# Fusion block on one core: GpSimd's row ids in four steps, a reciprocal on VectorE, and two VectorE steps put elsewhere in the turn

## The chip, the cores and the metric

The kernel runs on one core of one Trainium2 chip. The metric is the device time of one execution in microseconds. Engines are named as the profile names them: PE is TensorE, DVE is VectorE, ACT is ScalarE, POOL is GpSimd, SP is SyncE.

## What is computed

The reference is one transformer block over 16 images with 128 text rows each; all arithmetic is fp32.

```python
h = tokenize(x)                      # 64 patches of 28x28x3 and a class row, times pos_embed
h = concatenate([h, txt], axis=1)    # 16 x 193 x 128
h = h + attn(layernorm(h))           # linear attention, elu + 1, rotation, 1/z, 3-tap conv
h = h + ffn(layernorm(h))            # 8 experts, each row goes to 2, and one shared expert
# in ffn:
scores = xt @ gate_w.T
_, idx = top_k(scores + biases, 2)
p = sigmoid(top_k(scores, 2)[0]);  p = p / sum(p)
```

With e1 = exp(-s1) and e2 = exp(-s2) the two shares are (1 + e2) and (1 + e1), each over (2 + e1 + e2). So a row needs two exponentials, one sum and one reciprocal.

## The kernel before, in words

The 16 images are worked on in G = 8 groups of two. A group has three row tiles of 128 rows (one of patches, two of text); one more tile holds all class rows. Each engine runs one instruction list, written out by hand, and engines wait for each other on counting semaphores. A waiting instruction holds up everything behind it on its engine.

The program has three stages. In the first, the loop `for i in range(1, G - 1)` on DVE (line 1125), ACT (643) and PE (1542) works one *turn* per group: group i is projected and attended, group i-1 gets its second norm (`second_rows`, `second_stats`), and group i-2 is routed. The last group follows behind the loop, in a *tail* that also starts the shared expert (`shared_up`, `shared_down`) and splits the expert weights into a rounded part and a remainder (`remainder_w13`). In the second stage PE runs 56 expert tiles, one after the other; in the third the results come back and are added.

What the change touches in a turn of DVE:

- `turn_parts(i)` and `turn(i)` (lines 942 and 951) build the rotated features `rr` with three instructions over 128x768: two products (L947, L949) and their sum (L956). PE's `sums` (L1450, L1452) waits for the sum.
- `patch_rows(i+1)` (L915) takes the next group's patch tokens out of PE's bank; `patch_stats(i+1)` (L890, L894) takes their mean and variance. From there the path is ACT `rstd1` (L522, L524), DVE `mean1` (L900), ACT `norm_patches` (L555) and, behind that on ACT, `key_sums` (L550), for which PE's `attend` (L1464) waits.
- `positions(i-2)` (L1052) sums the places of group i-2's rows in the expert buffers.
- `attended` and `mixed` (L987, L992) end the attention of group i-1; `elu_most(i)` (L933) opens group i.

POOL works group by group. `goals(g)` writes the ids of the rows, `shares(g)` their weights (groups 0 to 5 only; `EARLIER` is 6), and then six indirect DMAs (L861; eight for the last group) scatter the rows to `xs_dram`. Inside `goals` and `shares` every step waits for the one ahead of it through `then_pool`, which counts them on `pool_chain`, 7 to a group (`WEIGHED`). ACT's `chances(g)` (L544) overwrites `odds` and waits until the group ahead has finished its 7. SP loads the first expert tiles once all 50 scatters have landed, and PE's expert loop begins with those tiles (L1658).

In the tail the order on DVE is `choices(5)`, `tap_before(7)`, `attended(6)`, `mixed(6)`, `elu_most(7)`, ..., `remainder_w13(0)`, `places(5)`, `positions(5)`, `remainder_w13(1)`, `attended(7)`, `mixed(7)`, `second_rows(7)` and so on to `positions(6)` and `positions(7)`.

Of the kernel before, what the change touches and what calls it, by code (L numbers as in the profile page):

```python
# [8 lines left out]
I32 = mybir.dt.int32  # L9
U32 = mybir.dt.uint32  # L10
ALU = mybir.AluOpType
# [3 lines left out]
P = 128  # L15
# [5 lines left out]
D = 128  # L21
# [4 lines left out]
G = B // 2  # L26
# [6 lines left out]
J = 3 * G + 1  # L33
CLS = J - 1
NID = J * P
EARLIER = G - 2
FROM = 3 * EARLIER
LATE = J - FROM
CAP = 3328
WEIGHED = 7  # L40
LARGEST = 1e30
TILES = (2 * NTOK - E) // P + E
ROW = D + 2
# [52 lines left out]
def destinations():  # L96

    flat = np.arange(J)[None, :, None] * P + np.arange(P)[:, None, None]
    ids = flat + np.arange(2)[None, None, :] * NID
    return np.concatenate([ids.reshape(P, 2 * J), np.full((P, 1), BIG)], 1).astype(np.int32)  # L100

def build(nc, patches, txt, w_tok, cls, pos, wqk, bqk, small, gate_b,
# [4 lines left out]
    with ctx:  # L108
# [11 lines left out]

        cst = sb("cst", [P, NCONST])
        ident, mask = cst[:, C_ID:C_ID + P], cst[:, C_MASK:C_MASK + P]
        dest_sb = sb("dest_sb", [P, 2 * J + 1], I32)
        wt = sb("wt", [P, KB, D])
        wt_rest = sb("wt_rest", [P, D])
        cols = sb("cols", [P, 4 + E])
# [61 lines left out]
        total = sb("total", [P, E], BF16)  # L188
        prod = sb("prod", [P, J, 2, E])
        pos_2 = sb("pos_2", [P, LATE, 2])  # L190
        apart = sb("apart", [P, 3], I32)
        chosen = sb("chosen", [P, 3, 2])
        crossed = sb("crossed", [P, 3])
        odds = sb("odds", [P, 3, 2])
        minus = sb("minus", [P, 3])
        odds_sum = sb("odds_sum", [P, 3])
        pos_i = sb("pos_i", [P, J, 2], I32)
        swap, keep = sb("swap", [P, LATE]), sb("keep", [P, LATE])
        part = sb("part", [P, 2, 2, LATE])
# [599 lines left out]
        def _(pool):  # L799
# [15 lines left out]
                                  dest_sb[:, 2 * FROM:2 * J].rearrange("p (j k o) -> p j k o", k=2, o=1)  # L815
                                  ).then_inc(ids_ready, 1)
            nc.gpsimd.memset(xd[:, FROM:, :, D + 1:D + 2], 1.0).then_inc(ids_ready, 1)
            nc.gpsimd.memset(minus[:], -1.0).then_inc(ids_ready, 1)
            pool.wait_ge(ids_ready, 3)

            ids = dest_sb[:, 0:2 * J].rearrange("p (j k) -> p j k", k=2)
            links = [0]

            def then_pool(ins):
# [4 lines left out]
            def goals(g):  # L829

                at = slice(3 * g, 3 * g + 3)
                pool.wait_ge(both_done, g + 1)
                then_pool(nc.gpsimd.tensor_copy(chosen[:], ix8[:, at, 0:2]))
                then_pool(nc.gpsimd.tensor_tensor(crossed[:], chosen[:, :, 0], chosen[:, :, 1], ALU.subtract))
                then_pool(nc.gpsimd.tensor_scalar(apart[:], crossed[:], 0.0, float(NID), ALU.is_gt, ALU.mult))
                nc.gpsimd.tensor_tensor(xd[:, at, 0, D].bitcast(I32), ids[:, at, 0], apart[:], ALU.add)
                nc.gpsimd.tensor_tensor(xd[:, at, 1, D].bitcast(I32), ids[:, at, 1], apart[:], ALU.subtract)

            def shares(g):

                at = slice(3 * g, 3 * g + 3)
                pool.wait_ge(odds_done, g + 1)
                then_pool(nc.gpsimd.tensor_scalar(odds[:], odds[:], LARGEST, 1.0, ALU.min, ALU.add))
                then_pool(nc.gpsimd.tensor_tensor(odds_sum[:], odds[:, :, 0], odds[:, :, 1], ALU.add))
                then_pool(nc.gpsimd.tensor_tensor(odds_sum[:], odds_sum[:], minus[:], ALU.pow))
                then_pool(nc.gpsimd.tensor_tensor(xd[:, at, :, D + 1], odds[:, :, ::-1], odds_sum[:].rearrange(
                    "p (t o) -> p t o", o=1).broadcast_to([P, 3, 2]), ALU.mult))

            for g in range(G):
                if g < EARLIER:  # L850
                    goals(g)
                    shares(g)

                pool.wait_ge(pos_done, g + 1)
                pool.wait_ge(x2_done, g + 2 if g == G - 1 else g + 1)
                if g == G - 1:
                    pool.wait_ge(twice_done, len(tiles_of(g)))
                for j in tiles_of(g):
                    rows = rows_of(j)
                    for k in range(2):  # L860
                        nc.gpsimd.indirect_dma_start(  # L861
                            out=xs_dram[:, :], out_offset=bass.IndirectOffsetOnAxis(ap=pos_i[0:rows, j, k:k + 1], axis=0),
                            in_=xd[0:rows, j, k, :], in_offset=None).then_inc(scattered, 16)
# [14 lines left out]
        def _(dve):  # L878
# [167 lines left out]
            def positions(g):  # L1046

                a, b = 3 * g, (J if g == G - 1 else 3 * g + 3)
                dve.wait_ge(pr_done, g + 1)
                with nc.allow_low_precision(reason="whole numbers below 2 ** 24"):  # L1050
                    if g < EARLIER:
# [73 lines left out]
            for i in range(1, G - 1):  # L1125
                if i > 1:
                    mean1(i)
                    heads(i - 1)
                    tap_behind(i - 1)
                    choices(i - 2)  # L1130
                    attended(i - 1)
                    mixed(i - 1)
                if i == 2:
                    text_stats(6)
                    text_stats(7)
# [7 lines left out]
                if i == 3:  # L1143
                    mean_texts(4, 4, G)
                turn_parts(i)
                turn(i)
                patch_rows(i + 1)
                patch_stats(i + 1)
                if i >= 2:
                    positions(i - 2)  # L1150
                tap_before(i)

            def shared_mul(c, m):
# [26 lines left out]
            tap_before(G - 1)  # L1180
            attended(G - 2)
            mixed(G - 2)
            elu_most(G - 1)
            elu_rest(G - 1)
            turn_parts(G - 1)
# [568 lines left out]
```

## Time and profile before

| what | before |
|---|---|
| runs (3) | 250.84, 250.85, 251.06 us; median 250.85 us |
| profiled execution | 250.12 us, span 248.3 us |
| granted clock, mean over the span | 0.987 |
| busy share of the span | PE 89%, DVE 75%, ACT 64%, POOL 54% |
| a turn of the loop, from the sums of one group to the next (turns 3 to 6) | 12.13 us |
| first scatter DMA / last scatter DMA / first expert tile on PE | 51.66 / 141.47 / 145.51 us |
| expert loop's own scatters (56) | 151.6 to 233.9 us |

The profiled execution is 0.73 us below the median of the runs. All times inside the kernel are from the start of the span.

### The profile page before, as it was taken

The numbers are of one execution on the slowest core, as the hardware profiler recorded it, in microseconds if no ns is written. First come the engines' busy times: TensorE is split into PE (matmuls) and PEld (weight loads), VectorE is DVE, ScalarE is ACT, GpSimd is POOL, SyncE is SP. The second block draws the span as 40 slices with busy tenths as digits, with TensorE's granted clock in tenths as the row PEclk, the third lists the DMA queues.
The fourth block names the chain that finished last, engine by engine and source line by source line (L and its number), as shares of the span: only waits on it lengthen the run. The fifth ranks groups of instructions, "written<-read, shape, count | busy, mean of one in ns | idle before, by whom it ended". The sixth has DMA issues, their size and how long they took to land.

```text
span 248.3 us, 5612 instructions
## 1 busy us (share of the span) xinstructions
PE 221.4 (89%) x1485; PEld 189.5 (76%) x1485; DVE 186.1 (75%) x706; ACT 159.4 (64%) x435; POOL 134.4 (54%) x178
## 2 busy tenths in 40 slices
PE   3898889999999999888989979999999999999930
PEld 2878778889898989756676658888888888887720
DVE  3548899998998989988977777666666666665760
ACT  3055676768687878869843266777777767776630
POOL 1400001258787778878777704666666666666500
PEclk9999999999999999999999999999999999999995
DMA  6999973142425101010113231423333333348657
GB/s 210 354 350 356 325 274 125 27 189 65 187 67 206 44 25 43 11 56 11 55 54 115 62 83 43 115 68 101 88 88 83 93 94 85 86 128 235 185 137 192
DMA packets 31566, 31.75 MB, mean 128 GB/s; under 512 B 4338, under 2 KB 27419, under 8 KB 30768
## 3 DMA queue, kind: packets, MB, share of 16 engines
q1 hardware_dynamic: 27240, 24.60, 32.7%
q0 software_dynamic: 3392, 6.38, 7.9%
q10 hardware_dynamic: 904, 0.41, 0.6%
q8 instruction: 13, 0.21, 0.4%
q14 instruction: 17, 0.14, 0.2%
HBM read 22.83 MB, written 9.06 MB: 128 GB/s over the span
## 4 chain that ended last, share of the span: by engine, by line
PE 57%; DVE 19%; issue 7%; ACT 6%; POOL 4%; DMA 4%; SPq 1%; DVEq 0%; POOLq 0%; ACTq 0%
PE bank L1669 15%; PE bank L1689 10%; PE bank L1678 5%; PE bank L1381 5%; POOL xs_dram L861 4%; DVE att L956 3%; DVE att L949 3%; DVE st L890 3%; PE bank L1658 3%; PE bank L1464 2%; PE bank L1450 2%; PE bank L1484 2%; DMA xp_both<-in_patches 2%; DVE hrow L998 2%; PE bank L1587 2%
## 5 line engine op out<-in xcount | busy, mean ns | idle before, releaser
L872 POOL DMA_INDIRECT y_dram<-att,goal x56 | 55.8, 996 | 35.8 <-ACT att L766 35.2
L861 POOL DMA_INDIRECT xs_dram<-xd,pos_i x50 | 52.2, 1044 | 21.8 <-issue 18.9
L1381 PE MATMUL bank<-wt,xp_both 128*128 128x128 f32 x288 | 40.7, 296 | 5.0 <-DMA xp_both<-in_patches 5.0
L1381 PEld LDWEIGHTS bank<-wt,xp_both 128*128 128x128 f32 x288 | 38.5, 208 | 6.3 <-DMA xp_both<-in_patches 5.3
L1689 PE MATMUL bank<-w_sb,att 128*128 x224 | 34.5, 277 | 0.0
L1298 DVE CAST xsT_h<-bank 128x128 fp32r<-128x128 f32 x56 | 16.3, 292 | 24.0 <-PE bank L1658 22.5
L752 ACT ACTIVATE att<-bank 128x256 f32<-128x256 f32 x56 | 21.5, 384 | 19.1 <-PE bank L1669 19.1
L1689 PEld LDWEIGHTS bank<-w_sb,att 128*128 128x128 f32 x224 | 29.4, 191 | 0.3 <-issue 0.2
L1669 PE MATMUL bank<-xp_both,xsT_h 128*128 x56 | 26.8, 479 | 0.0
L1311 DVE TENSOR_TENSOR att<-att,bank 128x256 f32<-128x256 f32 x56 | 23.2, 414 | 1.6 <-ACT att L752 1.6
L766 ACT ACTIVATE att<-bank,goal 128x128 f32<-128x128 f32 x56 | 20.6, 368 | 4.6 <-PE bank L1689 0.5
L1669 PE MATMUL bank<-xp_both,xsT_l 128*128 x56 | 22.1, 394 | 0.0
L1669 PE MATMUL bank<-w,xsT_h 128*128 x56 | 21.9, 392 | 0.0
L1678 PE MATMUL bank<-cst,att 128*128 128x128 f32 x112 | 21.5, 274 | 0.4 <-DVE att L1311 0.4
L759 ACT COPY att<-bank 128x256 f32<-128x256 f32 x56 | 20.9, 372 | 0.8 <-PE bank L1678 0.7
L1678 PEld LDWEIGHTS bank<-cst,att 128*128 128x128 f32 x112 | 13.8, 140 | 5.8 <-DVE att L1311 1.4
L1300 DVE TENSOR_TENSOR xsT_l<-bank,xsT_h 128x128 fp32r<-128x128 f32 x56 | 16.3, 292 | 1.9
L675 ACT ACTIVATE sh_s<-bank 128x384 f32<-128x384 f32 (+1 forms) x18 | 8.0, 456 | 13.3 <-PE bank L1575 12.4
L1658 PE MATMUL bank<-cst,xs_all 128*128 128x128 f32 x56 | 15.3, 273 | 1.4 <-DMA xs_all<-xs_dram 1.4
L1307 DVE COPY goal<-xs_all 128x2 f32<-128x2 f32 x56 | 14.9, 267 | 0.0
L1587 PEld LDWEIGHTS bank<-sw_sb,sh_h 128*128 128x128 f32 (+1 forms) x88 | 10.4, 187 | 5.2 <-DVE hrow L1165 2.2
L1572 PE MATMUL bank<-x2T,sw 128*128 128x384 f32 (+1 forms) x36 | 13.9, 467 | 0.4 <-DVE sh_h L1159 0.4
(225 smaller groups left out, 512.2 us busy)
## 6 DMA issues: line engine op xcount, KB each, us to landing
xp_both<-in_patches SPq DMA_DIRECT2D x6, 1152.0 KB
xs_all<-xs_dram SPq DMA_DIRECT2D x56, 65.0 KB, 1.9
xd<-y_dram SPq DMA_DIRECT2D x8, 384.0 KB, 5.1
w<-in_w SPq DMA_DIRECT2D x2, 1024.0 KB, 10.4
y_dram<-att,goal POOLq DMA_INDIRECT x56, 2.3
xs_dram<-xd,pos_i POOLq DMA_INDIRECT x50
xp_both<-in_patches SPq DMA_DIRECT2D x1, 768.0 KB, 5.4
hrow<-in_txt SPq DMA_DIRECT2D x2, 384.0 KB, 7.3
```

Source lines behind the costliest of these rows:

```text
L752: A(hs[q][:], bank[2 + q][:, 0:HID], ACT.Silu).then_inc(silu_done[at], 1)
L759: nc.scalar.copy(hmT[q][:], bank[4 + q][:, 0:HID].rearrange("p (m t) -> p m t", m=2)).then_inc(hmT_done[at], 1)
L766: A(ys[buf][:], bank[6 + q][:, 0:D], ACT.Copy, scale=goal[buf][:, 1:2]).then_inc(ys_done[at], 1)
L861: nc.gpsimd.indirect_dma_start(out=xs_dram[:, :], out_offset=bass.IndirectOffsetOnAxis(ap=pos_i[0:rows, j, k:k + 1], axis=0), in_=xd[0:row ...
L872: nc.gpsimd.indirect_dma_start(out=y_dram[:, :], out_offset=bass.IndirectOffsetOnAxis(ap=goal[u][:, 0:1].bitcast(I32), axis=0), in_=ys[u][ ...
L1298: V.tensor_copy(xsT_h[q][:], bank[q][:, 0:P]).then_inc(xh_done, 1)
L1311: V.tensor_tensor(hm[q][:], hs[q][:], bank[2 + q][:, HID:2 * HID], ALU.mult).then_inc(hm_done[at], 1)
L1381: M(ps[:, 0:D], xp[p][:, k, :], wt[:, k, :], start=(k == 0), stop=False)
L1658: T(bank[q][:, 0:P], xs[u][:, 0:D], ident).then_inc(tx_done[slot(u, 0)], 1)
L1669: last = M(bank[2 + q][:, 0:2 * HID], x[q][:], w[:, bass.ds(first * 2, 2 * HID)], start=(i == 0), stop=(i == 2))
L1678: last = T(bank[4 + q][:, P * m:P * m + P], hm[q][:, P * m:P * m + P], ident)
L1689: last = M(bank[6 + q][:, 0:D], hmT[q][:, m, :], w[:, bass.ds(first + m * D, D)], start=(m == 0), stop=(m == 1))
```

## The change

Four things are changed.

1. `goals`: the constant table `dest_sb` gets a second part with each row's flat id twice, `crossed` is computed for both slots at once (first minus second, second minus first), and one addition over 128x6 takes the place of an addition and a subtraction over 128x3. Four steps instead of five.
2. `shares`: POOL's power step (the sum to the power -1, L845) goes. DVE computes the reciprocal into a new tile `odds_part` at the head of `positions(g)`, behind a wait for POOL's sum; POOL's product waits for it. `WEIGHED` is 6, `SUMMED` is 5, and `pos_done` rises by two for groups 0 to 5.
3. `positions` is called a turn later: in the loop `positions(i-3)` behind `mixed(i-1)` and ahead of `elu_most(i)`, instead of `positions(i-2)` behind `patch_stats`; in the tail `positions(4)` comes behind `mixed(6)`. The calls for groups 5, 6 and 7 stay where they are.
4. `patch_rows(i+1)` is called ahead of `turn(i)` instead of behind it.

```diff
-WEIGHED = 7
+WEIGHED = 6
+SUMMED = 5
...
     ids = flat + np.arange(2)[None, None, :] * NID
-    return np.concatenate([ids.reshape(P, 2 * J), np.full((P, 1), BIG)], 1).astype(np.int32)
+    flat = np.broadcast_to(flat, ids.shape)
+    return np.concatenate([ids.reshape(P, 2 * J), np.full((P, 1), BIG), flat.reshape(P, 2 * J)], 1).astype(np.int32)
...
-        odds_sum = sb("odds_sum", [P, 3])
+        odds_sum, odds_part = sb("odds_sum", [P, 3]), sb("odds_part", [P, 3])
...
-                then_pool(nc.gpsimd.tensor_tensor(crossed[:], chosen[:, :, 0], chosen[:, :, 1], ALU.subtract))
+                then_pool(nc.gpsimd.tensor_tensor(crossed[:], chosen[:], chosen[:, :, ::-1], ALU.subtract))
                 then_pool(nc.gpsimd.tensor_scalar(apart[:], crossed[:], 0.0, float(NID), ALU.is_gt, ALU.mult))
-                nc.gpsimd.tensor_tensor(xd[:, at, 0, D].bitcast(I32), ids[:, at, 0], apart[:], ALU.add)
-                nc.gpsimd.tensor_tensor(xd[:, at, 1, D].bitcast(I32), ids[:, at, 1], apart[:], ALU.subtract)
+                nc.gpsimd.tensor_tensor(xd[:, at, :, D].bitcast(I32), ids[:, at, :], apart[:], ALU.add)
...
                 then_pool(nc.gpsimd.tensor_tensor(odds_sum[:], odds[:, :, 0], odds[:, :, 1], ALU.add))
-                then_pool(nc.gpsimd.tensor_tensor(odds_sum[:], odds_sum[:], minus[:], ALU.pow))
-                then_pool(nc.gpsimd.tensor_tensor(xd[:, at, :, D + 1], odds[:, :, ::-1], odds_sum[:].rearrange(
+                pool.wait_ge(pos_done, 2 * g + 1)
+                then_pool(nc.gpsimd.tensor_tensor(xd[:, at, :, D + 1], odds[:, :, ::-1], odds_part[:].rearrange(
...
-                pool.wait_ge(pos_done, g + 1)
+                pool.wait_ge(pos_done, g + 1 + min(g + 1, EARLIER))
...
             def positions(g):
+                if g < EARLIER:
+                    dve.wait_ge(pool_chain, WEIGHED * g + SUMMED)
+                    V.reciprocal(odds_part[:], odds_sum[:]).then_inc(pos_done, 1)
...
                     mixed(i - 1)
+                if i >= 3:
+                    positions(i - 3)
...
                 turn_parts(i)
+                patch_rows(i + 1)
                 turn(i)
-                patch_rows(i + 1)
                 patch_stats(i + 1)
-                if i >= 2:
-                    positions(i - 2)
                 tap_before(i)
...
             mixed(G - 2)
+            positions(G - 4)
```

DVE at the end of a turn of the loop: `att` is the rotation's three tiles, `hrow` the token rows, `st` and `mv` their statistics, `pos_i` the places, `hl` the convolution. Before:

```order
L947 TENSOR_TENSOR att<-att,sinx 128x768 [waits ftb_done,fta_done]
L949 TENSOR_TENSOR att<-att,cosx 128x768
L956 TENSOR_TENSOR att<-att 128x768
L915 TENSOR_TENSOR hrow<-bank,posb 128x128
L890 BN_STATS st<-hrow 128x6
L894 BN_AGGR mv<-st 128x2
L1052 TENSOR_REDUCE pos_i<-prod 128x6
L974 SCALAR_TENSOR_TENSOR hl<-xT,cols,hl 128x384
```

With the change:

```order
L946 TENSOR_TENSOR att<-att,sinx 128x768 [waits ftb_done,fta_done]
L948 TENSOR_TENSOR att<-att,cosx 128x768
L914 TENSOR_TENSOR hrow<-bank,posb 128x128 [waits tok_done]
L955 TENSOR_TENSOR att<-att 128x768 [waits qrT_done,kv_done,cs_done]
L889 BN_STATS st<-hrow 128x6 [waits hp_done]
L893 BN_AGGR mv<-st 128x2 [waits bs1]
L973 SCALAR_TENSOR_TENSOR hl<-xT,cols,hl 128x384 [waits lc_done]
```

The patch rows stand between the products and their sum, and the places' sum is gone from this spot.

DVE in the tail, from the multiplication of group 5's places (`prod`) to the end of the last group's attention (`ot`, `s_all`); `w` is the remainder of the expert weights. Before:

```order
L1042 TENSOR_TENSOR prod<-pick,bank 128x48 [waits place_done]
L1052 TENSOR_REDUCE pos_i<-prod 128x6 [waits pr_done]
L1174 TENSOR_TENSOR w<-w,xp_both 128x512 [waits wh_done]
L987 TENSOR_TENSOR ot<-bank,zr 128x386 [waits num_done,zr_done]
L992 TENSOR_TENSOR s_all<-ot,hl 128x386 [waits hl_done,ot_done]
```

With the change:

```order
L1041 TENSOR_TENSOR prod<-pick,bank 128x48 [waits place_done]
L1050 RECIPROCAL odds_part<-odds_sum 128x3 [waits pool_chain]
L1054 TENSOR_REDUCE pos_i<-prod 128x6 [waits pr_done]
L1176 TENSOR_TENSOR w<-w,xp_both 128x512 [waits wh_done]
L986 TENSOR_TENSOR ot<-bank,zr 128x386 [waits num_done,zr_done]
L991 TENSOR_TENSOR s_all<-ot,hl 128x386 [waits hl_done,ot_done]
```

A reciprocal that waits for POOL's count now stands ahead of the last group's attention.

POOL, one group. Before:

```order
L833 CAST chosen<-ix 128x6 [waits both_done]
L834 TENSOR_TENSOR crossed<-chosen 128x3 [waits pool_chain]
L835 TENSOR_SCALAR apart<-crossed 128x3 [waits pool_chain]
L836 TENSOR_TENSOR xd<-dest_sb,apart 128x3 [waits pool_chain]
L837 TENSOR_TENSOR xd<-dest_sb,apart 128x3
L843 TENSOR_SCALAR odds<-odds 128x6 [waits odds_done]
L844 TENSOR_TENSOR odds_sum<-odds 128x3 [waits pool_chain]
L845 TENSOR_TENSOR odds_sum<-odds_sum,minus 128x3 [waits pool_chain]
L846 TENSOR_TENSOR xd<-odds,odds_sum 128x6 [waits pool_chain]
L861 DMA xs_dram<-xd,pos_i 26752x130 [waits x2_done,pos_done,pool_chain]
```

With the change:

```order
L833 CAST chosen<-ix 128x6 [waits both_done]
L834 TENSOR_TENSOR crossed<-chosen 128x6 [waits pool_chain]
L835 TENSOR_SCALAR apart<-crossed 128x6 [waits pool_chain]
L836 TENSOR_TENSOR xd<-dest_sb,apart 128x6 [waits pool_chain]
L842 TENSOR_SCALAR odds<-odds 128x6 [waits odds_done]
L843 TENSOR_TENSOR odds_sum<-odds 128x3 [waits pool_chain]
L845 TENSOR_TENSOR xd<-odds,odds_part 128x6 [waits pos_done,pool_chain]
L860 DMA xs_dram<-xd,pos_i 26752x130 [waits x2_done,pos_done,pool_chain]
```

Two instructions are gone, and the product (L845 of the new numbering) waits for DVE's `pos_done`.

## Rows read from the trace of the kernel before

**Rows 1.** The page, part 1: busy us, share of the span and instructions.
```profile
PE 221.4 (89%) x1485; PEld 189.5 (76%) x1485; DVE 186.1 (75%) x706; ACT 159.4 (64%) x435; POOL 134.4 (54%) x178
```

**Rows 2.** Chain that ended last, in order of time: start us, us, what.
```profile
128.52 0.96 POOL xs_dram L861
...
141.47 1.94 DMA xs_dram<-xd,pos_i
```

**Rows 3.** DVE timeline, turn 6: start us, us, instruction, [idle before it <- releaser].
```profile
92.88 0.69 DVE L933 SCALAR_TENSOR_TENSOR att<-att,bank 128x512 f32<-128x512 f32 x1 [0.27 <-ACT att L495]
...
96.81 0.95 DVE L949 TENSOR_TENSOR att<-att,cosx 128x768 f32<-128x768 f32 x1
97.79 0.96 DVE L956 TENSOR_TENSOR att<-att 128x768 f32<-128x768 f32 x1
98.67 0.28 DVE L915 TENSOR_TENSOR hrow<-bank,posb 128x128 f32<-128x128 f32 x1
98.99 0.29 DVE L890 BATCH_NORM_STATS2 st<-hrow 128x6 f32<-128x128 f32 x1
99.31 0.18 DVE L894 BATCH_NORM_AGGREGATE mv<-st 128x2 f32<-128x6 f32 x1
```

**Rows 4.** ACT timeline, the same turn.
```profile
99.53 0.20 ACT L522 ACTIVATE lv<-mv 128x1 f32<-128x1 f32 x1 [0.28 <-DVE mv L894]
...
100.61 0.68 ACT L550 ACTIVATE ksm<-cst,kst 128x128 f32<-128x128 f32 x2
```

**Rows 5.** PE timeline, the same turn.
```profile
98.80 0.70 PE L1450 MATMUL bank<-xm,att 128*128 128x256 f32 x2
99.34 0.61 PE L1452 MATMUL bank<-xrow,att 128*128 128x128 f32 x4
...
101.55 0.92 PE L1464 MATMUL bank<-qq,ksm 128*128 128x193 f32 x4 [0.24 <-ACT ksm L550]
```

**Rows 6.** POOL timeline, ids and shares of group 0.
```profile
41.75 0.19 POOL L833 CAST chosen<-ix 128x6 f32<-128x6 uint32 x1 [22.05 <-DVE bc L1034]
...
43.06 0.19 POOL L837 TENSOR_TENSOR xd<-dest_sb,apart 128x3 int32<-128x3 int32 x1
44.04 0.26 POOL L843 TENSOR_SCALAR odds<-odds 128x6 f32<-128x6 f32 x1 [0.79 <-ACT odds L544]
...
44.66 0.90 POOL L845 TENSOR_TENSOR odds_sum<-odds_sum,minus 128x3 f32<-128x3 f32 x1
```

**Rows 7.** DVE timeline, the tail.
```profile
105.03 0.68 DVE L933 SCALAR_TENSOR_TENSOR att<-att,bank 128x512 f32<-128x512 f32 x1
...
113.12 0.20 DVE L1052 TENSOR_REDUCE pos_i<-prod 128x6 int32<-128x48 f32 x1
...
114.44 0.56 DVE L987 TENSOR_TENSOR ot<-bank,zr 128x386 f32<-128x386 f32 x1 [0.51 <-ACT zr L473]
...
123.34 0.15 DVE L1057 TENSOR_REDUCE pos_i<-pos 128x3 int32<-128x6 f32 x1
```

**Rows 8.** POOL timeline, scatters of groups 3 to 7.
```profile
98.02 1.56 POOL L861 DMA_INDIRECT xs_dram<-xd,pos_i  x1 [0.30 <-issue]
...
104.22 1.15 POOL L861 DMA_INDIRECT xs_dram<-xd,pos_i  x1 [0.30 <-POOL xd L846]
...
111.74 0.20 POOL L833 CAST chosen<-ix 128x6 f32<-128x6 uint32 x1
...
114.67 0.90 POOL L845 TENSOR_TENSOR odds_sum<-odds_sum,minus 128x3 f32<-128x3 f32 x1
...
124.33 1.35 POOL L861 DMA_INDIRECT xs_dram<-xd,pos_i  x1 [0.30 <-issue]
...
132.32 0.96 POOL L861 DMA_INDIRECT xs_dram<-xd,pos_i  x1 [0.30 <-issue]
```

**Rows 9.** PE timeline, the first expert tile.
```profile
145.51 0.30 PE L1658 MATMUL bank<-cst,xs_all 128*128 128x128 f32 x1 [0.65 <-DMA xs_all<-xs_dram]
```

**Rows 10.** DVE timeline, the kernel's one early reciprocal, over 14 columns.
```profile
149.92 0.23 DVE L1283 RECIPROCAL sg<-sg 128x14 f32<-128x14 f32 x1
```

More of the change, by code:

```diff
@@ L122, in build @@
         ident, mask = cst[:, C_ID:C_ID + P], cst[:, C_MASK:C_MASK + P]
-        dest_sb = sb("dest_sb", [P, 2 * J + 1], I32)
+        dest_sb = sb("dest_sb", [P, 4 * J + 1], I32)
         wt = sb("wt", [P, KB, D])
@@ L190, in build @@
         pos_2 = sb("pos_2", [P, LATE, 2])
-        apart = sb("apart", [P, 3], I32)
+        apart = sb("apart", [P, 3, 2], I32)
         chosen = sb("chosen", [P, 3, 2])
-        crossed = sb("crossed", [P, 3])
+        crossed = sb("crossed", [P, 3, 2])
         odds = sb("odds", [P, 3, 2])
-        minus = sb("minus", [P, 3])
-        odds_sum = sb("odds_sum", [P, 3])
+        odds_sum, odds_part = sb("odds_sum", [P, 3]), sb("odds_part", [P, 3])
         pos_i = sb("pos_i", [P, J, 2], I32)
@@ L817, in _ @@
             nc.gpsimd.memset(xd[:, FROM:, :, D + 1:D + 2], 1.0).then_inc(ids_ready, 1)
-            nc.gpsimd.memset(minus[:], -1.0).then_inc(ids_ready, 1)
-            pool.wait_ge(ids_ready, 3)
-            ids = dest_sb[:, 0:2 * J].rearrange("p (j k) -> p j k", k=2)
+            pool.wait_ge(ids_ready, 2)
+            ids = dest_sb[:, 2 * J + 1:4 * J + 1].rearrange("p (j k) -> p j k", k=2)
             links = [0]
```

## Prediction

> **What bounds the kernel now.** I read the page first, then the chain of waits in order of time, then the timelines of DVE, ACT, PE and POOL over one turn and over the tail. On the page PE is busy for 89% of the span and POOL for 54% [rows 1]. That does not say which of them sets the time in a stage, so the chain comes next. In the turns it runs from PE's sums to PE's `attend`, on to the mixed rows, through DVE to the rotation's sum, and back to PE's sums. From 128.52 us to the start of the expert loop it is POOL's scatters and, behind the last of them at 141.47, their landing and the load of the first tiles [rows 2]. PE takes the first expert tile at 145.51 and had waited 0.65 us for it [rows 9]. From there on PE's 56 tiles set the pace, and the change touches nothing there. So the change is worth what it moves that start of 145.51.
>
> Two places matter. The first is the turn. PE's `attend` starts at 101.55 and waited 0.24 us for ACT's `ksm` [rows 5]. ACT wrote `ksm` at 100.61, behind the patch rows' norm, and that began at 99.53, having waited 0.28 us for DVE's patch statistics [rows 4], which end at 99.31 + 0.18 = 99.49 [rows 3]. The second is POOL: from 51.66 on it goes from one scatter to the next without a stop, one group behind DVE. In the tail group 4's scatters begin at 104.22, group 5's ids at 111.74, its sum is ready when the power step begins at 114.67, and groups 6 and 7 are scattered from 124.33 and 132.32 on [rows 8].
>
> **Patch rows ahead of the sum: a gain of 1.3 us.** Before, L949 starts at 96.81, the sum at 97.79, the patch rows at 98.67 and their statistics at 98.99 [rows 3]. Each of the last two stands about 0.1 us behind the point where DVE was free, since it waits for the result just ahead of it. With the patch rows between the products and the sum both gaps are filled: patch rows at 97.68, sum at 97.89, statistics at 97.89 + 0.88 = 98.77. The sum is 0.10 us later and the statistics 0.22 us earlier. PE's sums start 0.10 later, and `kst` with them, which waits for L1452's end at 99.34 + 0.61 [rows 5]; that still comes ahead of ACT's new time for `ksm`, 100.39. So `attend` starts about 0.22 us earlier in every turn. The bounds are 0.10 us, were only the gap ahead of the statistics to count, and 0.24 us, PE's whole wait. Six turns give 6 x 0.22 = 1.3 us at the end of the loop.
>
> **Positions a turn later, in the loop: nothing.** The reciprocal and the sum of places now stand behind `mixed`, where DVE sat idle for 0.27 us until ACT's exponentials [rows 3]. The only early reciprocal in the trace takes 0.23 us over 14 columns [rows 10], a reduction of places 0.20 us [rows 7], and small instructions overlap their neighbours, so the two need about 0.2 us. If the cover were gone they would cost that in four turns, 0.8 us. ACT's `chances` of the next group now waits for a product a turn later; that product is ready about 0.5 us behind `mixed`, when ACT is still at its exponentials, so nothing is late behind it.
>
> **POOL's steps: nothing by themselves.** The power step is 0.90 us [rows 6, 8] and the fifth id step 0.19 us [rows 6], five times each behind the first scatter: 5 x 1.09 = 5.5 us of POOL's own time. But a group's scatter now cannot begin before DVE reaches `positions` a turn later, so POOL no longer runs at its own pace but at DVE's. The saving is what lets it keep up.
>
> **The new wait in the tail: a loss of 2.0 us.** `positions(5)` stays where it was, but `positions(4)` has moved to behind `mixed(6)`, and between the two POOL must scatter a whole group and prepare the next.
>
> 1. DVE reaches `positions(4)` where `elu_most(7)` stood, 105.03 [rows 7], less 1.32: 103.71.
> 2. Reciprocal 0.2, signal 0.1, product 0.2, and 0.30 from the product to the first DMA as in the row at 104.22: 0.8 us.
> 3. Six scatters. Group 4 took 111.74 - 104.22 = 7.52 us [rows 8] with none held up. A scatter that starts while DVE adds two tiles in SBUF is held: the one at 98.02 started inside L956 [rows 3], ended 0.91 us behind the start of the next DVE instruction, and took 1.56 us where others take 0.96 [rows 8]. On the new times the scatters of group 4 meet L949, L956 and the convolution's second tap, all three close to an edge. I take one hold, 0.7 us: 8.2 us. The bounds are none (7.5) and two full ones (8.9).
> 4. Ids and sum of group 5: 43.06 - 41.75 = 1.3 us for the four steps and 44.66 - 44.04 = 0.6 us for the clamp and the sum with its signal [rows 6]: 1.9 us. DVE stands still then, so nothing holds these up.
>
> That is 103.71 + 0.8 + 8.2 + 1.9 = 114.6. DVE would be at `positions(5)` at 113.12 - 1.32 = 111.8 [rows 7], so it waits 2.8 us. Behind it are the reciprocal, the reduction and one remainder, 0.8 us, and then `attended(7)` at 115.4 instead of 114.44 [rows 7]. The last group's attention, and with it the second rows, the routing of groups 6 and 7 and PE's work between them, comes 1.0 us *later*, though the loop ended 1.3 us earlier.
>
> **From there to the expert loop.** Group 6's places were ready at 123.34 + 0.15 and its first scatter started at 124.33, since POOL was still busy [rows 7, 8]. Now POOL is waiting and follows 0.3 us behind them, or 0.9 us if it is held by DVE's next instructions. So the last scatter moves by 1.0 less 0.54, or 1.0 plus 0.06; I take the middle, 1.0 - 0.25 = 0.75 us. PE's shared work in front of the loop moves by 1.0 and had 0.65 to spare, so it does not decide.
>
> **The sum** is 250.12 + 0.75 = 250.9 us for the profiled execution. That one stands 0.73 us below the median of the runs, so I expect a median of 251.6 us. A difference of 0.2%, 0.5 us, is about what a measurement of this kernel can tell from no change.
>
> By the Trainium skill ("SBUF — State Buffer", Who interferes with whom) an elementwise VectorE instruction with two SBUF inputs holds up GpSimd's reads but, as is inferred there, not its making of DMA descriptors. By that rule no scatter of group 4 would be held, and the time would be that of the second rival below. The row at 98.02 speaks against it.
>
> **The rivals.**
>
> *Faster: POOL arrives nearly in time.* If no scatter is held (7.5 us) and steps 2 and 4 take 0.3 us less each, the sum is ready at 113.3 and `attended(7)` starts at 114.1, 0.3 us earlier than before; with POOL's quick start for group 6 the last scatter moves by -0.3 - 0.54, about -0.8 us: 250.0. It decides from 113.6 on. For it: POOL has fewer steps and DVE is idle beside the last of them. Against it: all three must be at their best.
>
> *No change: no scatter of group 4 is held.* The sum is ready at 113.9, `attended(7)` moves by +0.3, the last scatter by -0.2 to +0.4: 250.9. For it: the same group ran without a hold before. Against it: it now starts half a microsecond nearer to DVE's three long instructions.
>
> *Much slower: the loop itself is caught.* A turn of POOL is now 0.8 + 8.2 + 1.9 = 10.9 us, with two holds more and a held id step up to 12.2 us, against a turn of DVE of 12.13 - 0.22 = 11.9. If POOL is the longer one, DVE waits 0.3 us in each turn ahead of `elu_most`, and the tail finds two holds: sum at 115.3 and up to 1.2 us behind it, so +1.8 to +3: 253. For it: the margin is small. Against it: DVE's idle 0.27 us takes the first part.
>
> *The change does not do what it says:* the patch rows could wait for PE's tokens and delay the sum. Against it: nothing on DVE waited at the patch rows [rows 3]; they would have to be 0.9 us late to matter as before.
>
> **How the numbers follow.** Forecast (one to two holds, +0.5 to +1.6) 0.40; no hold, no change 0.32 with what of the forecast falls under 0.5 us; much slower 0.10; faster 0.18. Slower is 0.40 + 0.10 = 0.50, same 0.32, faster 0.18. The range goes from the lower part of the faster rival, -0.85 us, to the worst sum with two holds and a held first scatter, +1.9 us: 250.0 to 252.8.
>
> **What would show it.** In the turns: statistics 0.2 us nearer to the products, no wait of `attend` on `ksm`, 11.9 us from sums to sums. In the tail: DVE idle ahead of the reciprocal of group 5 for 2 to 3.5 us with POOL's sum as its releaser; POOL idle ahead of group 6's scatter. I am wrong if that idle time is under 1.5 us, or if the turns do not shrink, or if the last scatter starts before 141.0.

## The result, and the profile after

The change makes the kernel slower: 252.36 us median against 250.76 us of the kernel before, 18 executions of each on one chip, a ratio of 1.0058 with an interval of 1.0035 to 1.0081, or 1.5 us (0.9 to 2.0). A second comparison gave 1.0082 (1.0051 to 1.0112). Forecast were 251.6 us, 0.75 us more than before the change, within 250.0 to 252.8, and "slower" as the likeliest case. The direction and the wait behind it came out as forecast. One step on the way was wrong, and one cause of the loss was not in the forecast at all.

The profiled execution shows almost none of the loss: 250.36 us, a span of 248.3 us as before the change. It is the fastest of the 18, and three things in it have to be told apart.

The page's busy times, to be held against [rows 1]: POOL has 8.8 us less to do, the others the same within 2.1 us.

```profile
PE 219.3 (88%) x1477; PEld 188.1 (76%) x1485; DVE 185.9 (75%) x712; ACT 159.7 (64%) x435; POOL 125.6 (51%) x165
```

**The turn is shorter, as forecast.** DVE's timeline, turn 6, answers to [rows 3]:

```profile
94.75 0.95 DVE L948 TENSOR_TENSOR att<-att,cosx 128x768 f32<-128x768 f32 x1
95.61 0.28 DVE L914 TENSOR_TENSOR hrow<-bank,posb 128x128 f32<-128x128 f32 x1
95.81 0.95 DVE L955 TENSOR_TENSOR att<-att 128x768 f32<-128x768 f32 x1
96.68 0.28 DVE L889 BATCH_NORM_STATS2 st<-hrow 128x6 f32<-128x128 f32 x1
97.00 0.18 DVE L893 BATCH_NORM_AGGREGATE mv<-st 128x2 f32<-128x6 f32 x1
```

From the start of the second product to the end of the statistics it takes 2.43 us, where it took 2.68; 0.22 was forecast, 0.25 came. PE's timeline answers to [rows 5]:

```profile
96.81 0.70 PE L1453 MATMUL bank<-xm,att 128*128 128x256 f32 x2
...
99.21 0.92 PE L1467 MATMUL bank<-qq,ksm 128*128 128x193 f32 x4
```

`attend` follows the sums by 2.40 us instead of 2.75 and no longer waits for `ksm`. A turn takes 11.85 us from sums to sums (the three from 61.26 to 96.81) instead of 12.13.

**The start of the execution differs by chance.** PE's first `sums`, after the change and (second fence) before it:

```profile
22.38 0.70 PE L1453 MATMUL bank<-xm,att 128*128 128x256 f32 x2 [0.81 <-DVE att L955]
```

```profile
23.08 0.70 PE L1450 MATMUL bank<-xm,att 128*128 128x256 f32 x2 [0.81 <-DVE att L956]
```

This is the loading stage, in which the change only makes one small table (`dest_sb`) larger, and five later traces with the same turns have these sums at 22.93 to 23.64, that of the same kernel at 23.03. So this execution is 0.7 us ahead before the changed loop begins. Counted from the first sums, the last sums of the loop come after 96.81 - 22.38 = 74.43 us, before the change after 98.80 - 23.08 = 75.72: the loop gives 1.3 us, as forecast.

**The tail gives it back.** DVE's timeline there, to be held against [rows 7]:

```profile
102.94 0.68 DVE L932 SCALAR_TENSOR_TENSOR att<-att,bank 128x512 f32<-128x512 f32 x1
...
113.62 0.18 DVE L1050 RECIPROCAL odds_part<-odds_sum 128x3 f32<-128x3 f32 x1 [2.57 <-POOL odds_sum L843]
...
114.40 0.55 DVE L986 TENSOR_TENSOR ot<-bank,zr 128x386 f32<-128x386 f32 x1
```

`elu_most` of the last group starts 2.1 us earlier than before, and the last attention only 0.04 us earlier: DVE stands still for 2.57 us ahead of the reciprocal of group 5. Its releaser is POOL, whose timeline answers to [rows 8]:

```profile
95.96 1.63 POOL L860 DMA_INDIRECT xs_dram<-xd,pos_i  x1 [0.30 <-issue]
97.90 0.96 POOL L860 DMA_INDIRECT xs_dram<-xd,pos_i  x1 [0.30 <-issue]
...
103.85 1.09 POOL L860 DMA_INDIRECT xs_dram<-xd,pos_i  x1 [0.57 <-POOL xd L845]
105.25 1.47 POOL L860 DMA_INDIRECT xs_dram<-xd,pos_i  x1 [0.30 <-issue]
...
111.83 0.21 POOL L833 CAST chosen<-ix 128x6 f32<-128x6 uint32 x1
...
113.39 0.20 POOL L843 TENSOR_TENSOR odds_sum<-odds 128x3 f32<-128x3 f32 x1
...
123.72 0.96 POOL L860 DMA_INDIRECT xs_dram<-xd,pos_i  x1 [1.47 <-DVE pos_i L1059]
...
140.37 0.85 POOL L860 DMA_INDIRECT xs_dram<-xd,pos_i  x1 [0.30 <-issue]
```

The first two rows are group 3's. Group 4's six scatters take 7.98 us with one of them held, that at 105.25 (8.2 with one held was forecast), ids and sum 1.76 (1.9 forecast). PE waits with DVE, and then starts the expert loop where it did before [rows 9]:

```profile
115.60 0.33 PE L1415 MATMUL bank<-cst,s_all 128*128 128x128 f32 x1 [1.99 <-DVE s_all L991]
...
143.35 1.50 PE L1590 MATMUL bank<-sw_sb,sh_h 128*128 128x128 f32 x12
145.50 0.41 PE L1661 MATMUL bank<-cst,xs_all 128*128 128x128 f32 x2 [0.65 <-issue]
```

As the times stand, the last scatter is 1.1 us earlier than before, and the start of 145.50 has not moved. With the 0.7 us of the start taken off, the last scatter is 0.4 us earlier (117.99 us behind the first sums against 118.39) and the expert loop begins 0.7 us later (123.12 us against 122.43). That start stands 0.65 us behind the end of PE's own shared work (143.35 + 1.50), with "issue" as the cause. Besides the wait for the tile's load, the program has between the two PE's wait for DVE's last shared multiplication (L1161, which ends at 144.63) and the loading of the first tiles' registers; what part of the 0.65 us each takes is not shown. The chain of waits agrees: before, it reached the loop over the scatters [rows 2], now over the shared expert's work, PE's products first and then ACT's and DVE's steps on the last of them. The longest pieces of it, in order of time:

```profile
133.24 1.56 PE bank L1590 x12
137.62 1.58 PE bank L1590 x12
139.58 0.71 PE bank L1575 x2
146.66 0.97 PE bank L1672 x3
```

So 0.7 us of loss show in front of the expert loop in this trace. That leaves about half of the measured loss to explain.

### The profile page after: what moved, and what is told of

Read it like the earlier page. It is cut to its first block, busy times and chain, and to the rows that moved or that the text cites. A ratio compares the mean times of both kernels' runs of the same rounds, so it can differ in the third digit from the quotient of the medians.

```text
span 248.3 us, 5603 instructions
## 1 busy us (share of the span) xinstructions
PE 219.3 (88%) x1477; PEld 188.1 (76%) x1485; DVE 185.9 (75%) x712; ACT 159.7 (64%) x435; POOL 125.6 (51%) x165
## 3 DMA queue, kind: packets, MB, share of 16 engines
q1 hardware_dynamic: 27240, 24.63, 32.7%
## 4 chain that ended last, share of the span: by engine, by line
PE 56%; DVE 25%; ACT 5%; issue 4%; POOL 3%; DMA 2%; SPq 1%; DVEq 1%; POOLq 0%; ACTq 0%
PE bank L1672 16%; PE bank L1692 10%; PE bank L1681 5%; PE bank L1590 4%; DVE st L889 3%; POOL xs_dram L860 3%; PE bank L1575 3%; DVE att L955 3%; DVE att L946 2%; PE bank L1661 2%; DMA cst<-in_consts 2%; PE bank L1578 2%; DVE att L948 2%; PE bank L1384 2%; PE bank L1453 2%
## 5 line engine op out<-in xcount | busy, mean ns | idle before, releaser
L860 POOL DMA_INDIRECT xs_dram<-xd,pos_i x50 | 54.1, 1083 | 18.2 <-issue 12.8
L1384 PE MATMUL bank<-wt,xp_both 128*128 128x128 f32 x288 | 39.9, 292 | 5.1 <-DMA xp_both<-in_patches 5.1
L1384 PEld LDWEIGHTS bank<-wt,xp_both 128*128 128x128 f32 x288 | 37.7, 205 | 6.5 <-DMA xp_both<-in_patches 5.4
L1575 PE MATMUL bank<-x2T,sw 128*128 128x384 f32 (+1 forms) x36 | 13.9, 467 | 0.4 <-DVE sh_h L1161 0.4
```

The lines of the kernel that those rows point to most:

```text
L860: nc.gpsimd.indirect_dma_start(out=xs_dram[:, :], out_offset=bass.IndirectOffsetOnAxis(ap=pos_i[0:rows, j, k:k + 1], axis=0), in_=xd[0:row ...
L1384: M(ps[:, 0:D], xp[p][:, k, :], wt[:, k, :], start=(k == 0), stop=False)
L1575: M(bank[second][:, 0:n], sw13[:, HID + P * m:HID + P * m + P], x, start=True, stop=True)
```

## The experiments

Two theories stood after the result. A: the wait ahead of the reciprocal is the whole loss. B: PE's idle time behind that wait also lets the granted clock fall in most executions, and the profiled one is an exception. What each run was to show was written down before it.

### Both kernels once more

No edit. For the changed kernel:

> The changed kernel once more, for a second trace. Its profiled execution of 250.36 us lies 2.0 us below its median, with the expert loop starting at 145.50 as before the change. Theory A (tail wait only): DVE's wait of 2.57 us ahead of the reciprocal of group 5 gives the loop's gain back and no more; then another execution shows the expert loop starting within 0.5 us of 145.5, and the 1.5 us of the median are lost elsewhere, behind 150 us. Theory B (clock): PE's idle time in the tail, now 1.99 us ahead of the mixed rows of the last group where it had less, lets the granted clock fall for a stretch; then this trace, if its time is near 252.4, shows a mean clock near 0.975, a stretch between 105 and 150 us with a granted clock of about a half, and the expert loop starting 1 to 3 us later than 145.5.

For the kernel before:

> The kernel before, once more, for the mean granted clock of all its executions. Theory B (clock): they stand at 0.985 to 0.99 in nearly all, and the time at 250.3 to 251.3 us. Theory A (the clock is no part of it): the clock varies here as it does with the change, 0.968 to 0.99, with no link to the time.

The changed kernel took 252.64 us (ratio 1.0082). This time the profile is of an ordinary execution, of 253.0 us. Its PE timeline in the tail:

```profile
116.28 0.47 PE L1415 MATMUL bank<-cst,s_all 128*128 128x128 f32 x1 [1.98 <-DVE s_all L991]
...
116.97 1.49 PE L1575 MATMUL bank<-x2T,sw 128*128 128x384 f32 x2
...
148.18 0.41 PE L1661 MATMUL bank<-cst,xs_all 128*128 128x128 f32 x2 [0.65 <-issue]
```

The pair of products L1575 takes 1.49 us where it took 0.81 at the same place of the first trace. The windows of the same trace name the reason; behind the stretch stand its length, PE's busy time with the number of its instructions, and the granted clock (1.00 is 2.4 GHz), then the DMA share and GB/s:

```profile
115.00:120.00 5.00, 3.72 (x9) 0.53 0.12 40
120.00:125.00 5.00, 5.00 (x25) 0.78 0.12 40
```

```profile
125.00:130.00 5.00, 4.21 (x29) 0.88 0.12 40
130.00:135.00 5.00, 5.00 (x20) 0.78 0.18 57
```

From `attended` of group 7 to the first expert tile it takes 32.7 us here (114.52 to 147.21), at full clock 31.1 (114.44 to 145.51): 1.6 us. Over all 104 executions of the kernel before that ran beside the experiments, 48 have a mean granted clock of 0.986 or more and a median of 250.1 us; 49 have 0.980 to 0.984 and 251.2 us; 7 have 0.977 and 251.0 us. Of the 30 executions of the changed kernel one has 0.990, five have 0.981 (251.7 us), 18 have 0.974 or 0.975 (252.5 us), and six less (254.5 us). My guess that nearly all executions of the kernel before stand at full clock was wrong: half of them do.

So B fits as far as the clock goes; the runs below test it. The wait costs too. `attended` of group 7, with the change and (second fence) before it:

```profile
115.07 0.56 DVE L986 TENSOR_TENSOR ot<-bank,zr 128x386 f32<-128x386 f32 x1
```

```profile
114.52 0.56 DVE L987 TENSOR_TENSOR ot<-bank,zr 128x386 f32<-128x386 f32 x1 [0.51 <-ACT zr L473]
```

The first sums are at 23.03 and 23.14 in these two traces, so it comes 0.66 us later counted from the sums. This is what is left of the wait's price once the loop's 1.3 us are taken off.

### The wait taken away

```diff
-            positions(G - 3)
             remainder_w13(1)
             attended(G - 1)
             mixed(G - 1)
+            positions(G - 3)
```

> The changed kernel with the reciprocal and the places of group 5 behind the last group's attention and mixing, in place of ahead of it. Theory A (tail wait): attended of group 7 starts near 112.4, when ACT's zr is there, and not at 114.40; group 5's scatters start as before near 114.8, POOL goes through groups 6 and 7 without a stop, the last scatter starts near 139.2 and the expert loop 1 to 1.5 us earlier than 145.5: 249.2 us for an execution like the profiled one. Theory B (clock): PE's idle 1.99 us falls to under 0.5 us, the mean clock goes back to 0.985 to 0.99 in nearly all executions, and the median falls by 2.5 to 3.5 us to about 249.3; if A alone holds the median falls by 1 to 1.5 us and the clock stays near 0.975.

Measured: 249.93 us, ratio 0.9965 (0.9937 to 0.9993) to the kernel before, 2.5 us under the changed kernel. DVE's timeline:

```profile
112.96 0.56 DVE L986 TENSOR_TENSOR ot<-bank,zr 128x386 f32<-128x386 f32 x1 [0.75 <-ACT zr L474]
...
114.54 0.18 DVE L1050 RECIPROCAL odds_part<-odds_sum 128x3 f32<-128x3 f32 x1 [0.43 <-POOL odds_sum L843]
```

The attention starts 2.1 us earlier than at 115.07 (2.0 counted from the sums, which are at 22.93), PE's idle 1.98 us is gone, and ten of twelve executions have a mean clock of 0.982 to 0.988. The expert loop starts at 144.60, now for the first tile's load:

```profile
144.60 0.33 PE L1661 MATMUL bank<-cst,xs_all 128*128 128x128 f32 x1 [0.70 <-DMA xs_all<-xs_dram]
```

So one call in the wrong place cost the change its gain. About 249.3 had been expected, with the clock at 0.985 or more in nearly all executions: the six at 0.987 or 0.988 have a median of 249.4, the other six, at 0.968 to 0.983, are slower.

### The wait kept, the idle time filled

This parts A from B: one product of 128x384, which PE needs next anyway, is run three times more into the same bank in the time in which PE would wait. DVE's wait stays.

```diff
             gate(G - 2)
+            pe.wait_ge(zl_done, G)
+            for _ in range(3):
+                M(bank[0][:, 0:3 * P], sw13[:, HID:HID + P], x2T[:, 0:3 * P], start=True, stop=True)
             mixed_rows(G - 1)
```

> The changed kernel with three more matmuls of 128x384 on PE between the gate of group 6 and the mixed rows of group 7. They repeat one that comes next, into the same bank, and add no result. DVE's wait of 2.57 us ahead of the reciprocal stays; only PE's idle 1.99 us behind it is filled. Theory B (clock): no stretch at the lower granted clock behind 115 us, the mean clock goes back to 0.98 to 0.99 in nearly all executions and the median falls by 1.5 to 2.5 us to about 250.5, though PE does more. Theory A (the wait alone): 252.5 us or more, since the same work still starts at the same time.

Measured: 252.55 us, ratio 1.0100 (1.0051 to 1.0150), of 6 executions. The clock behind 115 us did as B said, the time did not. The trace's windows, as above:

```profile
115.00:120.00 5.00, 4.93 (x20) 1.00 0.12 40
...
125.00:130.00 5.00, 4.16 (x32) 0.88 0.16 53
130.00:135.00 5.00, 5.00 (x20) 0.77 0.08 27
```

The fall at 115 us is gone. In its place is the one at 128 us that the kernel before also has, and all six executions have a mean clock of 0.981 to 0.984. So the fillers only exchanged one low stretch for another, of about the same price (2.0 and 1.6 us in the traces above).

The next run fills both places; half of a shared product is moved in front of the gate of group 7, where PE waited 0.58 us. The three repeated products stay as they are and are left out of the cut; `up_second(c, m)` is the second product of `shared_up(c, m)`, which `early=True` leaves out at its old place.

```diff
             turn_second(G - 1)
+            after(pe, sh_mul, 4)
+            up_second(3, 0)
             gate(G - 1)
             shared_down(2)
-            shared_up(3, 0)
+            shared_up(3, 0, early=True)
```

> The changed kernel with both idle stretches of PE in the tail filled: the three repeated matmuls ahead of the mixed rows of group 7, and half of a shared product moved in front of the gate of group 7. Before this run the account is: the turns give 1.3 us, the wait ahead of the last attention takes 1.9 us, which makes +0.6 us, and the lower clock takes the rest. If that holds, the mean clock is 0.985 to 0.99 in most executions and the median is the 250.1 us that the kernel before shows in its executions at 0.987 and above, plus 0.6: 250.5 to 251.0. If the wait alone is the loss, it stays at 252.5.

Measured: 250.60 us, ratio 0.9988 (0.9966 to 1.0010), ten of twelve executions at 0.983 to 0.990. DVE's wait is still 2.55 us in this trace, and its windows:

```profile
115.00:120.00 5.00, 5.00 (x18) 1.00 0.09 27
...
130.00:135.00 5.00, 4.86 (x29) 1.00 0.26 79
```

With the same wait and a full clock in the tail the loss falls to 0.5 us against the 250.1 us of the kernel before at full clock, within the 250.5 to 251.0 us that were expected. The half product itself also shortens PE's work: counted from the first sums, the expert loop starts after 146.42 - 23.64 = 122.78 us, 0.34 us earlier than in the first trace with the change. So the loss is a little less than the 0.66 us of the wait. That is the account: the wait less the loop's gain 0.7 us, the clock the rest.

The half product alone, on the kernel before:

> The kernel before with nothing but the half product moved in front of the gate of group 7, where PE had 0.58 us of idle time. If the clock's fall behind that gate comes of the idle time and the narrow matmuls around it, the executions at 0.983, now half of all, are gone: the clock is 0.987 to 0.99 and the median 250.0 us or less, with 0.2 to 0.6 us from PE's shorter work. If not, the clock is 0.983 in half of them as before and the median 250.2.

Measured: 250.19 us, ratio 0.9981 (0.9960 to 1.0001), no clear gain. Executions at 0.977 to 0.983 are still there, five of twelve, and they should have been gone if that gate were the only place of the fall; the profiled one had 0.990, so where their low stretch lies is open. In its trace PE has 0.79 us of idle time ahead of the first tile, more than the usual 0.65, so there the load seems to set the start and a shorter PE to buy little. Both of PE's idle stretches filled with real halves, on top of the variant without the wait:

> The variant with group 5's places behind the last mixing, and two halves of the shared expert's products moved into PE's two idle stretches in front of the gates of group 6 (idle 0.75 us) and of group 7 (idle 0.58 us). Theory B: the stretch at the lower clock that the kernel before shows behind the gate of group 7 goes as well; the mean clock is 0.987 to 0.99 in nearly all executions and the median 249.2 to 249.5 us, 0.5 us below that variant. PE's shared work in front of the expert loop also ends up to 1.2 us earlier, but POOL's last scatter and its landing then set the start, so an execution at full clock gains 0 to 0.4 us. Rival: the lower clock has nothing to do with these short stretches, and the median stays at 249.9.

Measured: 249.99 us, ratio 0.9995 (0.9961 to 1.0030), no better than the 249.93 us (0.9965) without the halves. Its expert loop starts at 144.61 against 144.60, and waits for the first tile's load: there POOL is the bound, and a shorter PE buys nothing. Four executions lie at 0.971 to 0.979 here as well.

### The parts alone

The changed kernel with the patch rows back behind the sum:

```diff
                 turn_parts(i)
+                turn(i)
                 patch_rows(i + 1)
-                turn(i)
```

> The changed kernel with the patch rows back behind the rotation's sum. By my prediction's step the patch rows alone are worth the 0.28 us of a turn: the turn goes back to 12.1 us, the loop ends 1.3 to 1.7 us later, and the sum of group 5 on POOL, which in the tail is DVE's releaser, comes later by nearly as much less what POOL no longer waits: attended of group 7 starts 1 to 1.7 us later than 114.40 and the median is about 253 to 254 us. Rival: POOL and DVE are in step through the reciprocal, and POOL sets the pace of the turn; then nothing moves and the median is 252.4.

Measured: 255.25 us, ratio 1.0173 (1.0111 to 1.0236), of 6 executions. From the first to the last sums of the loop it takes 75.62 us (23.37 to 98.99), as before the change. So the whole gain of the turn is the patch rows', and the later places cost the loop nothing. It came out over 1 us slower than expected, with a granted clock of 0.73 to 0.93 in six of the seven windows of 5 us from 105 to 140 us.

The other way round, the kernel before with this move alone:

> The kernel before with nothing but the patch rows ahead of the rotation's sum. By my prediction's step: attend starts 0.22 to 0.28 us earlier in each of six turns, the loop ends 1.3 to 1.7 us earlier, POOL has one group at 12.3 to 13.0 us and falls behind DVE, so that group 7's scatters start at most 0.5 us earlier than at 132.32: 249.9 to 250.9 us. Rival: POOL's pace is the whole bound in the tail and there is no gain: 250.8 us with the loop's end 1.5 us earlier. Second rival: the turn owes its gain to the places' sum having gone from behind the statistics, not to the patch rows: then the turn stays at 12.1 us.

Measured: 250.77 us, ratio 0.9990 (0.9956 to 1.0024). The four turns from 52.50 to 100.33 take 11.96 us each, before the change 12.22. Five executions at a mean clock of 0.984 to 0.986 took 248.7 to 249.9 us, so at full clock some of the gain arrives; the other seven, at 0.971 to 0.978, took 250.4 to 252.8. The profiled one is of these. Its clock is low from 38 to 45 us, and POOL is late at the end: the last scatter starts at 143.97, and PE waits for it.

```profile
148.19 0.33 PE L1658 MATMUL bank<-cst,xs_all 128*128 128x128 f32 x1 [2.08 <-DMA xs_all<-xs_dram]
```

So the rival is right for such executions, in which POOL cannot catch up; for the others no trace shows it. The ids in four steps alone:

> The kernel before with nothing but the ids in four steps. By my prediction's step POOL saves about 0.2 us in each of six groups, which it can use since it goes from scatter to scatter without a stop behind group 0: the last scatter comes up to 1.2 us earlier than 141.47. But PE's shared work ends at 144.87 as before and the expert loop starts 0.65 us behind it: 250.5 us, no change. Rival: the scatters set the start of the expert loop, and it comes 0.5 to 1.2 us earlier: 249.3 to 250.0.

Measured: 250.84 us, ratio 1.0035 (1.0006 to 1.0065). POOL's and PE's timelines of that trace:

```profile
140.37 0.84 POOL L861 DMA_INDIRECT xs_dram<-xd,pos_i  x1 [0.30 <-issue]
```

```profile
145.58 0.41 PE L1658 MATMUL bank<-cst,xs_all 128*128 128x128 f32 x2 [0.65 <-issue]
```

With the first sums at 23.04, as before, the last scatter is 1.1 us earlier and the expert loop is not. In the kernel before, PE's shared work set that start just as the scatters did. Why the median is a little above that of the kernel before, its trace doesn't show.

Patch rows and four steps together, with the power step left on POOL:

> The kernel before with the patch rows ahead of the sum and the ids in four steps; power step and places as before, so that DVE waits for POOL nowhere. By the account so far the turns shrink to 11.9 us as with the whole change, POOL keeps up since the ids' steps have shown that they save more than 0.2 us in a group, attended of group 7 starts 1.3 us earlier than before the change, and the shared work with it: 249.0 to 249.4 us. Rival: POOL's turn is over 11.9 us with the power step in it, it falls behind, and its last scatter sets the start of the expert loop: 249.8 to 250.5.

Measured: 250.35 us, ratio 0.9966 (0.9941 to 0.9991). Three executions lie at 0.988 to 0.990 and 248.5 to 249.1 us, as fast as expected or faster; the other nine at 0.969 to 0.981. Its trace has the low stretch where that of the patch rows alone had it:

```profile
36.00:38.00 2.00, 1.35 (x8) 1.00 0.83 323
38.00:40.00 2.00, 2.00 (x13) 0.52 0.57 234
40.00:42.00 2.00, 2.00 (x9) 0.50 0.00 0
```

Yet POOL keeps up: the last scatter starts 119.24 us behind the first sums, where it took 120.49 with the patch rows alone, and PE has only the usual 0.65 us of idle time where it had 2.08.

```profile
146.38 0.32 PE L1658 MATMUL bank<-cst,xs_all 128*128 128x128 f32 x1 [0.65 <-DMA xs_all<-xs_dram]
```

So in this pair of traces it takes the four steps for the patch rows' gain to reach the expert loop.

The last run fills that place too, and the one at the gate of group 7. The cut has the first; the second is the half product as above:

```diff
                 turn_queries(i - 1)
+                if i == 2:
+                    pe.wait_ge(zl_done, 1)
+                    M(bank[5][:, 0:2 * D], xT[1][:, 2:2 + P], wqk_sb[:], start=True, stop=True)
                 turn_second(i - 2)
+                if i == 2:
+                    M(bank[5][:, 0:2 * D], xT[1][:, 2:2 + P], wqk_sb[:], start=True, stop=True)
                 sums(i - 1)
```

> Patch rows ahead of the sum and ids in four steps, with PE's idle stretches filled at two places: the half product in front of the gate of group 7, and two repeated matmuls of 128x256 around 36 us, where PE waits 0.48 and 0.65 us and behind which the trace without them has a granted clock of a half from 38 to 45 us. If the idle time around 36 us is what lets the clock fall there, its executions near 0.974 are gone, the clock is 0.985 to 0.99 in nearly all, and the median is 248.6 to 249.1 us, where that variant's executions at 0.988 and above lay. If the fall has another cause, the two levels stay, 0.974 and 0.989, and the median is 249.8 to 250.4.

Measured: 249.45 us, ratio 0.9947 (0.9918 to 0.9976), the lowest median and ratio of all kernels here, though the interval overlaps that of the variant without the wait. The same windows:

```profile
36.00:38.00 2.00, 1.79 (x10) 1.00 0.73 300
38.00:40.00 2.00, 2.00 (x19) 1.00 0.62 257
```

The fall behind 36 us is gone, and in all twelve executions the clock is 0.977 or more. Eight of them still have 0.977 to 0.981; the profiled one, of 0.981, has its low stretch at the first expert tiles, between 145 and 150 us. So 248.6 was not reached.

## Why the prediction was right, and where it was not

- **Patch rows, 1.3 us.** Right in cause: 75.72 - 74.43 = 1.3 us, 0.35 us less between sums and `attend`, and gone when the patch rows go back. That the sum fits so well is in part luck: forecast were six turns of 0.22 us, but the first turn got longer by 0.08 us (14.11 against 14.03) and the other five gained 0.25 to 0.29 us each.
- **Places a turn later, nothing.** Right: with them and without the patch rows the loop takes 75.62 us.
- **The wait in the tail.** Right: 2.57 us against a forecast of 2.8; one scatter held, as taken. `attended` of group 7 came 0.66 us later instead of 1.0: the scatters (7.98 for 8.2) and the ids (1.76 for 1.9) were both a little shorter than taken. Two further misses cancel: from the reciprocal to the first scatter it takes 1.09 us for 0.8, but the reciprocal came 0.25 us earlier than taken. The heading calls the loss 2.0 us, while the working under it (1.0 us later in spite of 1.3 us gained) gives 2.3; counted from the sums, the wait cost 2.0 us (92.04 against 90.03 us without it). The "no hold" that the Trainium skill's "SBUF — State Buffer", Who interferes with whom, infers for descriptor making is again not what the trace shows: the scatter at 95.96, in POOL's timeline above, takes 1.63 us, against 0.96 for the one behind it, and ends at 97.59, 0.91 us behind the start of L889, the instruction that follows DVE's sum of two tiles.
- **"PE's shared work had 0.65 to spare, so it does not decide."** This step failed. I read the 0.65 us ahead of the first expert tile [rows 9] as slack, since the profile puts it down to a load. It is there at full and at low clock, in both kernels, 0.64 to 0.65 us behind the end of PE's last shared product, and it stayed when four steps alone brought the scatters 1.1 us earlier. So PE's shared work decides, and it moved by the 0.7 us by which DVE was late. The last scatter, on which I had based the sum (+0.75 us), moved the other way, by -0.40 us from the first sums: group 6's first scatter came 0.09 us later, that of group 7 had to wait 0.3 us more for its places, and the two scatters that took 1.35 us before, at 124.33 [rows 8] and 138.64, now took 0.96. That the expert loop moved by about the 0.75 us forecast is luck.
- **"The last scatter starts before 141.0: then I am wrong."** It did, at 140.37; by my own test that step was wrong. 0.70 us of that is the early start of the execution, but counted from the sums, too, the scatter came earlier and not later.
- **The clock was missing.** The forecast has no term for it, because the profile of the kernel before shows a granted clock of 1.0 until the last slices. With the account of the runs, 250.1 us at full clock, plus 0.66 for the wait, plus 2.0 for the low stretch makes 252.8; the changed kernel measured 252.4 to 252.6. The kernel before pays 1.1 to 1.6 us in half of its executions. So the median moved by 1.5 us, twice the forecast 0.75, and it lies within the range only because the upper bound had been set by another loss, two held scatters, that did not come.
- **Much slower, the loop caught by POOL.** Not in the loop: DVE has no idle time ahead of the reciprocal there.

## What to carry to other kernels

When a step is delayed on one engine and its successor stays where it was, count what the other engine must do between the two: one group's six scatters between two calls was 2.6 us of standing still, and moving the successor three calls down brought the work behind it 2.0 us forward. An idle time ahead of a matmul is slack only if it shrinks when the transfer named there comes earlier; look for the same gap in traces where another thing came last. And one profiled execution is one draw: hold its start and its granted clock against those of the other executions before a difference of 1% is read out of it.

## What was not expected of the hardware

- In the tail PE's granted clock fell to 1.2 GHz, from about 115 to 122 us, behind 1.98 us of idle time, itself shortly behind a wait of 0.74 us and a gate of narrow matmuls; in the first trace of the same kernel, with 1.99 us idle at the same place, it did not fall. One such stretch cost 1.6 to 2.0 us of the kernel's time.
- In the trace of each run that filled an idle place at which a trace had shown the fall (115 us, 128 us, 38 us), the clock stayed at 2.4 GHz there; in two of them it fell later, behind 128 and behind 145 us. There is one trace for each of these runs, and the fall comes and goes between executions of one kernel. In the variant of two parts the clock fell behind 36 to 38 us with PE busy for 1.35 of 2.00 us, and in the changed kernel's second trace it did not with 1.36. What decides between the two is open.
